# Neighbour gathers of graph layers 1 to 3 written out on GpSimd, their indices read from the stored row numbers

## What is computed

```python
h = relu(layernorm(x))
x = x + L0(h, edge_index, ...)                       # attention over edges
h = relu(layernorm(x))
# layer 1: message = g * xj[dst], summed into src
pxj = (edge_attr_64 @ Wdesc.T) * xj_all[idx_j];  xj = segment_sum(pxj, idx_i)
...
# layer 2: v = x[src] @ top + x[dst] @ bottom, layer norm, relu, times a weight, summed into dst
em = relu(layer_norm(concat(x[src], x[dst]) @ msg_w + msg_b)) * edge_weight;  msgs = segment_sum(em, dst)
...
# layer 3: a filter from edge_attr_50 and edge_attr_3 times x[dst] @ lin1, summed into src
W = (ssp(edge_attr @ mlp_w1.T + mlp_b1) @ mlp_w2.T + mlp_b2) * C;  agg = segment_sum(W * (x[j] @ lin1_w.T), i)
```

## Time and profile before

| | |
|---|---|
| median of 3 runs | 7043.58 us (7038.37 to 7045.12) |
| the profiled execution | 7035.33 us, its span 7033.4 us |
| busy in the span | PE 4579.0, DVE 4606.7, POOL 4416.4, ACT 2601.2 us |
| edge phase of layer 1, first to last gather | 3299.9 to 4338.7 us |
| edge phase of layer 2, first to last gather | 4647.3 to 5747.7 us |
| edge phase of layer 3, first to last gather | 5919.4 to 6968.8 us |

### The profile page before, as it was taken

One profiled execution on the slowest core, in us unless ns is written; L12 is line 12 of the kernel. 1 busy time (PEld: TensorE's weight loads), 2 busy tenths in 40 slices (PEclk: granted clock), 3 DMA queues, 4 the chain that ended last, 5 costly groups with the idle time before them and its releaser, 6 DMA issues. The chain is left out here.

```text
span 7033.4 us, 132070 instructions
## 1 busy us (share of the span) xinstructions
PE 4579.0 (65%) x25390; PEld 3559.5 (51%) x25391; DVE 4606.7 (65%) x15350; ACT 2601.2 (37%) x6676; POOL 4416.4 (63%) x4764
## 2 busy tenths in 40 slices
PE   5777777404555554664666666666766666899897
PEld 4566666303444444553555554245555544666664
DVE  8777777444444444666555556877777776777776
ACT  2355555202222224665000003833333334444443
POOL 0077777726777775555777775047777752777774
PEclk9988888755555556776666666888888876877877
DMA  1154444521222223441333332023223221333332
GB/s 62 33 149 148 148 148 147 89 41 43 58 58 58 58 58 96 118 118 48 79 79 79 79 79 50 0 66 74 75 74 74 73 50 48 72 73 72 72 72 60
DMA packets 858676, 541.10 MB, mean 77 GB/s; under 512 B 652276, under 2 KB 757576, under 8 KB 858184
## 3 DMA queue, kind: packets, MB, share of 16 engines
q1 hardware_dynamic: 710536, 239.88, 15.6%
q0 software_dynamic: 148032, 300.00, 15.4%
HBM read 411.68 MB, written 127.68 MB: 77 GB/s over the span
## 5 line engine op out<-in xcount | busy, mean ns | idle before, releaser
L1333 POOL DMA_INDIRECT l2e_rows<-l_rows,l2e_idx x832 | 847.2, 1018 | 561.8 <-DVE l2e_idx L1341 322.9
L1333 POOL DMA_INDIRECT l3e_rows<-l_rows,l3e_idx x832 | 796.1, 957 | 425.0 <-DVE l3e_idx L1341 216.5
L1201 POOL DMA_INDIRECT dst_rows<-l0d_out,l0d_idx x832 | 804.3, 967 | 277.2 <-issue 196.1
L1333 POOL DMA_INDIRECT l1e_rows<-l_rows,l1e_idx x832 | 785.5, 944 | 306.2 <-issue 193.9
L813 POOL DMA_INDIRECT src_records<-sort_rec,sort_idx x784 | 780.4, 995 | 312.1 <-issue 229.9
L2155 PE MATMUL l2e_pV<-l2e_rows,ident 128*128 128x512 f32 x416 | 297.5, 805 | 359.7 <-DMA l2e_rows<-l_rows,l2e_idx 359.3
L1173 PE MATMUL l0d_pX<-table,l0d_ohT 128*128 x1664 | 463.0, 459 | 85.8 <-issue 66.6
L1173 PEld LDWEIGHTS l0d_pX<-table,l0d_ohT 128*128 128x128 f32 x1664 | 394.5, 327 | 139.8 <-issue 139.8
L1315 PE MATMUL l0m_pR<-l0m_rows,l0m_oh 128*128 128x129 f32 x1664 | 319.2, 356 | 213.6 <-DVE acc L1283 139.5
L1508 PE MATMUL l1e_pG<-k_weights,l1e_dT 64*128 64x128 f32 x1664 | 217.8, 399 | 368.3 <-DVE l1e_prod L1537 365.2
L1528 ACT ACTIVATE l1e_dT<-l1e_pD 128x256 f32<-128x256 f32 x208 | 79.9, 384 | 956.8 <-PE l1e_pD L1497 941.0
(11 more groups left out here) (416 smaller groups left out, 13649.1 us busy)
## 6 DMA issues: line engine op xcount, KB each, us to landing
sort_rows<-lo_rows SPq DMA_DIRECT2D x196, 256.0 KB
sort_rec<-rec SPq DMA_DIRECT2D x98, 472.0 KB
l0m_rows<-dst_rows SPq DMA_DIRECT2D x416, 66.0 KB, 2.1
l0m_rows<-dst_rows POOLq DMA_DIRECT2D x416, 66.0 KB
l1e_rec<-src_records SPq DMA_DIRECT2D x832, 32.0 KB
l2e_lrow<-dst_local SPq DMA_DIRECT2D x208, 128.0 KB
l3e_rec<-src_records SPq DMA_DIRECT2D x832, 25.0 KB
l0d_meta<-src_records SPq DMA_DIRECT2D x832, 6.0 KB
```

The source lines that it names most:

```text
L1201: e.indirect_dma_start(kn.by_dst[:, :], bass.IndirectOffsetOnAxis(ap=r["idx"][:, st.quad, j:j + 1], axis=0), r["out"][:, st.quad, j, :], N ...
L1333: e.indirect_dma_start(r["rows"][:, st.quad, j, 0:width], None, table[:, :], bass.IndirectOffsetOnAxis(ap=r["idx"][:, st.quad, j:j + 1], a ...
```

## The change

The loop of gathers on POOL becomes straight code. It takes its indices from `kn.dst_of` and `kn.src_of` where they stand, so the copies on DVE, their ring and the semaphore `idx_ok` go. In layers 1 and 3 the ring of rows has eight buffers instead of four, in layer 3 inside the tile `spare` (`kn.MT`), and the rounds of DVE, which must name the buffer, are now unrolled eight times there instead of four (by `RING` in place of `QUAD`). In layer 2 the ring stays at four.

```diff
-def gather_stage(kn, e, r, table, width, used):
-
-    def gather(st):
-        wait_step(e, r["idx_ok"], st)
-        wait_step(e, used, st, 4)
+def gather_rows(kn, e, r, table, width, columns, used, ring=4):
+
+    for i in range(STEPS):
+        if i >= ring:
+            e.wait_ge(used, i - ring + 1)
         take_waits(e, kn.tally)
         for j in range(G):
-            e.indirect_dma_start(r["rows"][:, st.quad, j, 0:width], None, table[:, :],
-                                 bass.IndirectOffsetOnAxis(ap=r["idx"][:, st.quad, j:j + 1], axis=0)
-                                 ).then_inc(r[f"got{st.quad}"], 16)
-    return gather
-
-def idx_stage(kn, e, r, columns):
-
-    def idx(st):
-        e.tensor_copy(r["idx"][:, st.quad, :], columns[:, bass.ds(st.i * G, G)]).then_inc(r["idx_ok"], 1)
-    return idx
+            e.indirect_dma_start(r["rows"][:, i % ring, j, 0:width], None, table[:, :],
+                                 bass.IndirectOffsetOnAxis(ap=columns[:, i * G + j:i * G + j + 1], axis=0)
+                                 ).then_inc(r[f"got{i % ring}"], 16)
...
-            run_steps(e, ch, [(gather_stage(kn, e, r, kn.l1_rows, H, r["prod_ok"]), 0)], STEPS, QUAD)
+            gather_rows(kn, e, r, kn.l1_rows, H, kn.dst_of, r["prod_ok"], RING)
...
-                wait_quad(e, r, "got", st, G)
+                e.wait_ge(r[f"got{st.ring}"], st.eighth * (16 * G) + 16 * G)
...
-                      + [(prod, 4), (idx_stage(kn, e, r, kn.dst_of), 0)], STEPS, QUAD)
+                      + [(prod, 4)], STEPS, RING)
...
-            run_steps(e, ch, [(gather_stage(kn, e, r, kn.l2_rows, H, r["v_ok"]), 0)], STEPS, QUAD)
+            gather_rows(kn, e, r, kn.l2_rows, H, kn.src_of, r["v_ok"])
...
-                      + [(scaled, 4), (idx_stage(kn, e, r, kn.src_of), 0), (turned, 1), (shifted, 4)], STEPS, QUAD)
+                      + [(scaled, 4), (turned, 1), (shifted, 4)], STEPS, QUAD)
...
+        r["rows"] = flat(kn, kn.MT)[:, 0:RING * G * H].rearrange("p (k j h) -> p k j h", k=RING, j=G)
...
-            run_steps(e, ch, [(gather_stage(kn, e, r, kn.l3_rows, H, r["prod_ok"]), 0)], STEPS, QUAD)
+            gather_rows(kn, e, r, kn.l3_rows, H, kn.dst_of, r["prod_ok"], RING)
...
-                      + [(prod, 6), (idx_stage(kn, e, r, kn.dst_of), 2)], STEPS, QUAD)
+                      + [(prod, 6)], STEPS, RING)
```

More of the change, by code:

```diff
@@ L1538, in prod @@
                                 r["pG"][:, st.par, :, 0:2 * P].rearrange("p q (u c) -> p q u c", u=2),
-                                r["rows"][:, st.quad, :, :].rearrange("p (u q) c -> p q u c", q=2), ALU.mult
+                                r["rows"][:, st.ring, :, :].rearrange("p (u q) c -> p q u c", q=2), ALU.mult
                                 ).then_inc(r["prod_ok"], 1)
             run_steps(e, ch, in_turn(add_stages(kn, e, ch, r, 1, 6), hot_stages(kn, e, ch, r, 1, 4, 2, 2))
-                      + [(prod, 4), (idx_stage(kn, e, r, kn.dst_of), 0)], STEPS, QUAD)
+                      + [(prod, 4)], STEPS, RING)
             e.wait_ge(r["added"], STEPS)
@@ L1546, in l1_edges @@
                                     ("pR", [P, 2, G, P], F32)],
[L1547 to L1550, removed]
+               sbufs=[("rec", [P, 4, G, A64], F32), ("oh", [P, 2, G, P], F32), ("rows", [P, RING, G, H], F32),
+                      ("dT", [P, 2, 2, P], F32), ("prod", [P, 2, G, P], F32)],
+               sems=["hot", "rec_turned", "dT_ok", "g_done", "prod_ok", "summed", "added"]
+               + [f"ld{j}" for j in range(4)] + [f"got{j}" for j in range(RING)])
 def l1_layers(kn):
@@ L2228, in l2_edges @@
                       ("oh", [P, 4, G, P], F32), ("z", [P, 4, G, H], F32), ("sq", [P, G, H], F32),
-                      ("var", [P, 2, G], F32), ("std", [P, 2, G], F32), ("rstd", [P, 2, G], F32), ("idx", [P, 4, G], I32)],
-               sems=["idx_ok", "turned", "v_ok", "squared", "std_ok", "scaled", "affine", "z_ok", "hot", "summed", "added"]
+                      ("var", [P, 2, G], F32), ("std", [P, 2, G], F32), ("rstd", [P, 2, G], F32)],
+               sems=["turned", "v_ok", "squared", "std_ok", "scaled", "affine", "z_ok", "hot", "summed", "added"]
                + [f"ld{j}" for j in range(4)] + [f"got{j}" for j in range(4)])
@@ L2322, in prod @@
             def prod(st):
-                wait_quad(e, r, "got", st, G)
+                e.wait_ge(r[f"got{st.ring}"], st.eighth * (16 * G) + 16 * G)
                 wait_step(e, r["w_ok"], st)
-                e.tensor_tensor(r["prod"][:, st.par, :, :], r["prod"][:, st.par, :, :], r["rows"][:, st.quad, :, :],
+                e.tensor_tensor(r["prod"][:, st.par, :, :], r["prod"][:, st.par, :, :], r["rows"][:, st.ring, :, :],
                                 ALU.mult).then_inc(r["prod_ok"], 1)
@@ L2336, in l3_edges @@
                                     ("pR", [P, 2, G, P], F32)],
-               sbufs=[("rec", [P, 4, G, wide], F32), ("oh", [P, 2, G, P], F32), ("rows", [P, 4, G, H], F32),
+               sbufs=[("rec", [P, 4, G, wide], F32), ("oh", [P, 2, G, P], F32),
                       ("dT", [P, 2, 2, P], F32), ("prod", [P, 2, G, P], F32), ("soft", [P, 2, BANK], F32),
-                      ("s", [P, 2, BANK], F32), ("idx", [P, 4, G], I32)],
+                      ("s", [P, 2, BANK], F32)],
                sems=["cleared", "hot", "even", "rec_turned", "dT_ok", "h_done", "log_ok", "s_ok",
-                     "w_done", "w_ok", "prod_ok", "idx_ok", "summed", "added"]
-               + [f"ld{j}" for j in range(4)] + [f"got{j}" for j in range(4)])
+                     "w_done", "w_ok", "prod_ok", "summed", "added"]
+               + [f"ld{j}" for j in range(4)] + [f"got{j}" for j in range(RING)])
 def l3_finish(kn):
```

## The result

The changed kernel takes 7022.5 us (median of 12 runs, 7012.7 to 7033.5), the kernel before 7040.9 us (12 runs). The ratio is 0.9972, 95% interval 0.9965 to 0.9979: 19.7 us less (15 to 25). I had forecast 11.6 us less, with a range of 7008 to 7054 us.

The account below looks back on a forecast made before the run. The prediction took POOL's gathers to bound all three edge phases. Head starts of -0.3, -0.3 and -8.0 us and -3 us for the copies sum to -11.6 us: 7043.6 becomes 7032 us, range 7008 to 7054 us.

Parts of the forecast that it names:

- POOL is the bound and the pace is 0.944 + 0.304 us, written out or not: All three edge phases: a gather takes 1.248 us, 832 take 1038 us; ending the loop gives 0.
- the rows with 1.00 and 1.01 us: Two groups of small-row, bounds-checking gathers; had their difference come from the index tile, 150 us more; prediction took 0.
- The head start, -8.6 us: Without `idx_ok` POOL begins at the barrier: -0.3 us each in layers 1 and 2, -8.0 us in layer 3.
- A ring of four would take back 5.5 of the 8 us, one of eight takes back nothing: Layer 3: late products would make POOL wait for buffers in a ring of four, not in one of eight.
- The copies on DVE, -3 us: Layer 2: without copies L2194 and L2219 start 0.06 to 0.07 us earlier, releasing some 80 lengthened gathers earlier; -3 us.
- the contention of layer 2 loosens: Rival, layer 2: the shift moves a third of the DVE-gather meetings out of the way; -29 us, 7014 us; chance 0.25.
- Layer 1, 0 us: Layer 1's gather stretch: no lengthened gathers, its product having only one input in SBUF; no change beyond the head start.
- The stretch of layer 3, 0 us: Layer 3, from first gather's start to last gather's end: no change forecast.
- The rival of a reload: Rival: DVE's loops of 506 and 603 instructions are loaded again each round; 58 us more, 7090 us; chance 0.07.
- the second case: Whole kernel: looser contention in layer 2, -14 to -45 us; chance 0.25.
- the first: Whole kernel: the forecast's own case, -3 to -14 us; chance 0.45.

Follow-up runs that it names:

- mix_a: Changed kernel with rings of four and DVE rounds unrolled four times in layers 1 and 3, one unused DVE copy in layer 2: ratio 1.0002 to the kernel before.
- l2_only: Kernel before with layer 2 alone changed (gathers written out, stored row numbers, no DVE copies there): ratio 0.9984, 11 us less.
- mix_b: Changed kernel with three unused DVE copies in layer 2 and DVE's rounds of layer 3 unrolled sixteen times: ratio 0.9982, 13 us less than the kernel before.

## Why the prediction was right or wrong

- **POOL is the bound and the pace is 0.944 + 0.304 us, written out or not.** Right: the median gather is 0.944 us in all layers, the mean gap 0.305, none over 0.32. The loop cost nothing and the index tile of 832 columns costs nothing; the rows with 1.00 and 1.01 us were rightly not taken.
- **The head start, -8.6 us.** Right to 0.1 us in all three layers. I forecast that the chain of layer 3 would be 18.5 us late at step 2 and in time at step 21. It was 18.8 us late and in time at step 15: it caught up by 1.4 us a step, not 1.
- **"A ring of four would take back 5.5 of the 8 us, one of eight takes back nothing."** The second half is right, the first is a term that was too small: 10.4 us. I took it from one profile of the chain's start, which scatters by some us (step 3 of `mix_a`, steps 3 to 5 of `l2_only`), and left out the 0.8 us between the product's end and the gather behind it (5947.69 to 5948.48). There are six waits, 12.4 us in all. That each wait also moves the rows of later steps while the chain is still late would explain the rest; it wasn't tested by itself. What the ring of eight is for is more than I wrote: even without a head start POOL once waited 2.7 us with a ring of four.
- **The copies on DVE, -3 us.** The place is right, the port and the copy ahead of L2194 and L2219. The step from there to a time is wrong, and the size too small by a factor of four or more (12 to 16.7 us). I multiplied some 80 meetings by the 0.07 us by which each would end earlier. What changed is how many there are: 66 and 54 with one copy, 33 and 34 without it. The rival "the contention of layer 2 loosens" had this, with -20.6 us for it, and I held against it that 0.07 us is little. But a meeting of 0.42 us that is entered or missed by a step of 0.07 us isn't small where both engines run in step with each other. My sign for the rival was a mean gather of 990 ns or less, for the forecast one near 1018. It is 998 (1008 in `l2_only`), between the two: by that sign alone neither case had come.
- **Layer 1, 0 us.** Wrong by +4.7 us. I saw no lengthening in it before and took that for a property of its product. In the changed kernel 125 gathers take 0.02 to 0.1 us more, all of them with L885 running at their start, where 6 did before. There the copy had stood behind the product and L866 began 0.99 us behind the product's start; now it begins 0.84 us behind it. Gathers that start while L885 runs have become more, 319 where there were 126, but most of them keep their 0.94 us. One of the lengthened ones:

```profile
3704.66 0.28 DVE L885 TENSOR_SCALAR l1e_oh<-iota,local 128x128 f32<-128x128 f32 x1
3704.76 0.99 POOL L1333 DMA_INDIRECT l1e_rows<-l_rows,k_dst_of  x1 [0.30 <-issue]
```

  `mix_a` excludes the ring and the rounds; that the shift alone does it was argued and not shown.
- **The stretch of layer 3, 0 us.** It is 2.3 us shorter, all of it fewer lengthened gathers (10.7 to 8.3 us). The profiles with copies there have 10.7 and 9.3 us of lengthening, those without 8.3, 6.4 and 5.5; no run tests it by itself where POOL is the bound.
- **The longer loops.** The rival of a reload fell: 67 to 93 packets is the new code, the 2895 instructions that POOL's program grows by are 23 of them at 128 each, and no branch costs more. The prediction counted 506 and 603 instructions in the built program. By the records of the trace, which are what is fetched, the loops have 213 and 245, and one of 246 had run in layer 0 before. So the rival rested on a wrong count, and it was no luck that it fell. The Trainium skill, Runtime: NRT & Kernel Launch, "Instruction fetch mechanics", gives most engines room for 512 instructions. By the records no DVE loop of the changed kernel exceeds that. The page's stall behind a taken branch is borne out by the loop of 486 records, which `mix_b` reloads in every round. That loop too is under 512, so the figure can't be taken for the length of a loop that stays. The packets of the queue in question (q14) are 8 KB, where the page has blocks of 16.
- **The sum.** The 19.7 us lie between my forecast of 11.6 and the 29 of the faster rival. By size and by mechanism it was the second case that came (-14 to -45 us), and I had put the first ahead of it with 0.45 to 0.25. That 7022.5 us lies in my range is owed to the range, which took in most of that case. That the sum came as near as 8 us is in part luck: layer 1 lost 4.7 us that I hadn't foreseen, a third of what layer 2 gave beyond my term. Only the head start came as its working said.

## What to carry to other kernels

Where one engine's steady row of instructions is the bound, read what runs on the engine that shares its port at the start of each, and count the meetings by their distance; here the loss of a copy that shifts the rest by 0.07 us went with half of them. Taking the cause away (one input from PSUM) was worth more than twice the whole change, and it doesn't depend on where the instructions fall. A head start is kept only if the ring spans the lag that it creates, waits and wake-ups counted. And the length of a loop is to be counted in the trace, not in the built program: for DVE's loops they differ by a factor of some 2.4.

## What the runs showed of the hardware that was not expected

- A DVE loop of 245 records in the trace runs with 0.22 us behind its branch and no packets of its own; one of 486 has 2.9 us in each round and five packets of 8 KB, one in 128 records. POOL's written-out gathers use a packet in 126 to 131 records.
- On two of the three chips of the experiments every kernel took 8.5 to 8.8 ms, and the timeline shows engines that go on long after what they wait for has ended. In the kernel before, on such a chip, PE has ended the transposes of a step at 4324.5 us and ACT takes them at 4334.7:

```profile
4324.15 0.38 PE L1497 MATMUL l1e_pD<-ident,l1e_rec 128*128 128x128 f32 x2
4334.70 0.38 ACT L1528 ACTIVATE l1e_dT<-l1e_pD 128x256 f32<-128x256 f32 x1 [12.25 <-DMA l0t_ml<-run_ml,l0t_at]
```

  SP, which waits for the same transposes ahead of its next loads, goes on at 4334.6 too. The gathers themselves keep 0.944 us there. Whether the signal comes late or the engines take it late, and why, no run tells. In the time between, SP's instructions stand 0.7 us apart instead of 0.1 to 0.4. The changed kernel, in which POOL waits for fewer engines, gains more on such a chip: 1.6% instead of 0.28%, and on the other one four kernels made from it 2.6 to 2.7%.
